# A third tap of layer 0's depthwise convolution moved to ScalarE, with an accumulating transfer in place of one add

## The chip, the cores and the metric

The kernel runs on one core of a Trainium2 chip. The metric is the device time of one execution in microseconds (us). All times are of float32 work: both layers compute in float32 (layer 1 splits its matmul operands into float32r halves).

## What is computed

The input x is (2, 768, 64, 64). Layer 0 is a gated state-space block on the group-normalised x, with 1536 inner channels (12 groups of 128):

```python
x = hs @ in_proj_w.T                       # 768 -> 1536 channels
xs = conv3x3_depthwise(x, conv_w) + conv_b # 9 taps for each channel, zero padding
xs = xs * sigmoid(xs)
dt, Bs, Cs = split(xs_seq @ x_proj_w.T, [R, R + DSTATE])   # R = 48, DSTATE = 4
delta = softplus(dt @ dt_w + dt_b)
states = scan over all 4096 positions of a*s + b, a = exp(delta * A), b = delta * u * Bs
y = sum over 4 states (states * Cs) + D * u
y = layernorm(y) * ln_g + ln_b
x = x + y @ out_proj_w.T                   # 1536 -> 768 channels
```

Layer 1 is a channel attention with two 768 x 768 projections. The change does not touch it.

## The kernel before

Layer 0 works in chunks of 8 image rows (512 positions): 8 chunks for each of 2 images, so 16 chunks, and in each chunk 12 tiles, one for each group of 128 inner channels. That makes 192 tiles of 128 x 512. The whole of layer 0 is one software pipeline written out by hand: `for S in range(SLOTS)`, where each engine has its own list of what it does in slot S. A tile goes through its steps at fixed distances. Tile i has its input projection in slot i, its convolution in slot i+2, the last adds of the convolution in slot i+3, the product with B in slot i+16, its scan in slot i+17, the sum over states in slot i+18, the statistics of the layer norm in slot i+19. The output projection of a chunk runs over slots 31 to 42 after the chunk's first slot. Each engine's queue is in order, and semaphores hold the engines together. In this text "slot 3" means a slot whose number leaves 3 when divided by 12; a chunk of 12 slots is a period in which everything recurs.

In one slot the engines do this:

- TensorE: the input projection of the new tile (6 matmuls, L564, into the one bank `p_in`), half an output projection (6 matmuls, L580, into the one bank `p_op`), in every second slot the sums of the layer norm. In slot 3 the small products that give dt, B and C (L675 just before it, L570, then L534); in slots 3, 7 and 11 the four products L534 that give dt for four tiles, in two pairs. The second pair waits until the first pair's softplus is done. Each output projection but the first waits until VectorE has taken the one before out of `p_op` (L952, `x_res`).
- VectorE: two scans (L917) and their products with C (L923), in odd slots the scaling of an output tile and the residual add (L945, L952), three convolution taps (L938), the two other scans and products, and three more taps, the last of which writes the sum to the tile's column of `uy`. In slot 8 it also works out the layer norm's factor.
- ScalarE: the centre tap, which starts the sum in the PSUM bank `p_cv` (L768); the square for the layer norm (L774); two taps as plain products into the buffer `conv_part` (CT, L715), with the skip product D * u (L785) between them; then the exponentials of the scan (L706, `p_da`, two before each pair of scans) and the copies of the scan's last state (L711). After them the copy of the new tile out of `p_in` (L739, L743, L747). In slots 2, 6 and 10 it applies SiLU to four tiles, in slots 3, 7 and 11 softplus to four tiles (L729), each with two loads of the function table.
- GpSimd: an accumulating transfer that adds two of the four states' products onto the other two (`g_ring`, L871, 512 KB), the two adds of ScalarE's products onto `uy` (L876, L879), delta * u (L883), its product with B for all four states (L889), and two more adds (L893, L897).

```python
def product(i, n):
    wait(act, s_conv, 2 * (i - 1) + n + 1)
    nc.scalar.activation(rows(CT[:, n]), win_view(i, 2, 1 + n), ACT.Copy,
                         scale=cwt[:, i % K, 7 + n:8 + n]).then_inc(s_ct, 1)
```

So each product waits until GpSimd has added the same product of the tile before. After ScalarE's part of slot S is done, VectorE's scans of slot S+1 can begin: the first exponential of the next tile (`decay(i, 0)`) is the last but one thing in ScalarE's slot.

## Time and profile before

| what | value |
|---|---|
| median of three runs | 3775.08 us (3770.55 to 3781.36) |
| the profiled execution: its own time, its span | 3775.21 us, 3773.4 us |
| TensorE busy over the span | 3440.0 us, 91% |
| VectorE | 2915.9 us, 77% |
| ScalarE | 2353.5 us, 62% |
| GpSimd | 2344.4 us, 62% |
| mean busy share of the DMA engines, layer 0 in its steady part | 0.55 |

The busy shares are means over both layers. Layer 0's pipeline runs from about 118 us to 2760 us of the span. Only there does the change act, and only while there are tiles to convolve, to about 2585 us. Times below are counted from the span's start. A row of the timeline has the start, the duration, engine, line, operation, the names and shapes, the count, and in brackets the idle time of that engine before it with what ended it.

### The profile page before, as it was taken

What the parts mean: (1) busy time and instruction counts of PE and PEld (TensorE: products, weight loads), DVE (VectorE), ACT (ScalarE), POOL (GpSimd) and SP (SyncE); (2) the same over time, 40 slices, a digit from 0 to 9 for tenths busy, and PEclk for the clock granted to TensorE, in tenths of its full rate; (3) what the DMA queues carried; (4) which work ended last, traced back from release to release, by engine and by line L of the source; (5) the groups of instructions that cost most, each with busy time, mean ns of one, the idle gap of its engine ahead of it and who ended that gap; (6) DMA issues with size and microseconds to landing.
All of it is one profiled execution on the core that took longest, in us unless ns stands there. A gap on an engine that the chain in (4) does not pass through costs nothing. (4 is left out here: it accounts for less than half of the span.)

```text
span 3773.4 us, 39046 instructions
## 1 busy us (share of the span) xinstructions
PE 3440.0 (91%) x10696; PEld 1731.0 (46%) x10696; DVE 2915.9 (77%) x4082; ACT 2353.5 (62%) x4094; POOL 2344.4 (62%) x1557
## 2 busy tenths in 40 slices
PE   4876799999999899999999999997879999999999
PEld 4422233333334344333333333332337867767787
DVE  4469999999999989999999999998743345555532
ACT  1356777788777767777777777777534555432211
POOL 0148888898889978988888889888820001112111
PEclk7888899999999999999999999998999999999999
DMA  7244455655556544555555555555532223356564
GB/s 281 88 143 107 102 139 132 166 137 144 145 130 170 131 126 133 144 147 146 150 134 144 147 147 149 136 140 156 130 108 78 65 82 99 111 185 198 198 195 154
DMA packets 217034, 529.85 MB, mean 140 GB/s; under 512 B 24728, under 2 KB 45784, under 8 KB 213872
## 3 DMA queue, kind: packets, MB, share of 16 engines
q1 hardware_dynamic: 173808, 376.32, 31.7%
q0 software_dynamic: 43008, 151.02, 18.3%
q8 instruction: 88, 1.44, 0.2%
q14 instruction: 130, 1.06, 0.1%
HBM read 346.11 MB, written 80.48 MB: 113 GB/s over the span
## 5 line engine op out<-in xcount | busy, mean ns | idle before, releaser
L564 PE MATMUL p_in<-xn,win_v 128*128 128x512 f32 (+1 forms) x2304 | 1062.5, 610 | 103.2 <-ACT halo L747 64.7
L580 PE MATMUL p_op<-uy,wout_ring 128*128 128x512 f32 x2160 | 1019.9, 622 | 83.4 <-DVE x_res L952 83.4
L917 DVE TENSOR_TENSOR_SCAN p_da<-p_da,state,g_ring 128x512 f32<-128x512 f32 x672 | 827.4, 1277 | 110.2 <-ACT p_da L706 74.6
L889 POOL TENSOR_TENSOR g_ring<-du,B_bc 128x2048 f32<-128x2048 f32 x192 | 870.6, 4534 | 15.9 <-DMA B_bc<-bc_scratch 0.9
L938 DVE SCALAR_TENSOR_TENSOR p_cv<-win_v,conv_w,p_cv 128x512 f32<-128x512 f32 x960 | 723.0, 753 | 88.5 <-ACT p_cv L768 67.5
L564 PEld LDWEIGHTS p_in<-xn,win_v 128*128 128x128 f32 x2304 | 442.2, 197 | 696.2 <-issue 696.2
L580 PEld LDWEIGHTS p_op<-uy,wout_ring 128*128 128x128 f32 x2160 | 413.5, 198 | 680.0 <-issue 568.1
L706 ACT ACTIVATE p_da<-delta,A 128x512 f32<-128x512 f32 x768 | 499.5, 682 | 12.5 <-ACT state L711 0.2
L923 DVE TENSOR_TENSOR g_ring<-p_da,C_bc 128x512 f32<-128x512 f32 x768 | 487.3, 676 | 0.0
L1370 PE MATMUL banks<-x_split,w_split 128*128 128x512 f32 x1152 | 464.2, 403 | 24.1 <-DMA ident<-in_ident_d 19.9
L1372 PE MATMUL banks<-x_split,w_split 128*128 128x512 f32 x1152 | 452.0, 392 | 0.0
L1371 PE MATMUL banks<-x_split,w_split 128*128 128x512 f32 x1152 | 451.5, 392 | 0.0
L876 POOL TENSOR_TENSOR uy<-uy,conv_part 128x512 f32<-128x512 f32 x192 | 256.0, 1333 | 259.2 <-DVE uy L938 259.2
L1215 POOL DMA_DIRECT2D q_scratch<-q_ring x96 | 51.9, 540 | 535.9 <-DVE q_ring L1635 535.7
L715 ACT ACTIVATE conv_part<-win_v,conv_w 128x512 f32<-128x512 f32 x384 | 273.4, 715 | 15.2 <-POOL uy L876 5.1
L1370 PEld LDWEIGHTS banks<-x_split,w_split 128*128 128x128 f32 x1152 | 218.0, 189 | 116.9 <-issue 38.9
L879 POOL TENSOR_TENSOR uy<-uy,conv_part 128x512 f32<-128x512 f32 x192 | 244.5, 1273 | 29.0 <-POOL uy L876 2.2
L711 ACT ACTIVATE state<-p_da 128x2 f32<-128x2 f32 x384 | 65.3, 170 | 304.3 <-DVE g_ring L923 301.9
L897 POOL TENSOR_TENSOR uy<-uy,g_ring 128x512 f32<-128x512 f32 x192 | 243.8, 1270 | 15.1
L893 POOL TENSOR_TENSOR g_ring<-g_ring 128x512 f32<-128x512 f32 x192 | 244.1, 1272 | 12.4 <-DMA g_ring<-g_ring 12.3
L883 POOL TENSOR_TENSOR du<-delta,uy 128x512 f32<-128x512 f32 x192 | 248.7, 1295 | 0.0
L1223 POOL DMA_DIRECT2D out<-x_ring x96 | 51.8, 540 | 311.1 <-DVE x_ring L1579 305.8
(212 smaller groups left out, 4283.6 us busy)
## 6 DMA issues: line engine op xcount, KB each, us to landing
g_ring<-g_ring POOLq DMA_DIRECT2D x192, 512.0 KB, 5.6
win_v<-in_win SPq DMA_DIRECT2D x192, 384.0 KB, 3.1
wout_ring<-wout_scratch SPq DMA_DIRECT2D x184, 384.0 KB, 4.0
x_ring<-x_scratch SPq DMA_DIRECT2D x192, 256.0 KB, 2.7
q_scratch<-q_ring POOLq DMA_DIRECT2D x96, 256.0 KB, 2.4
x_split<-q_scratch SPq DMA_DIRECT2D x96, 256.0 KB, 3.3
out<-x_ring POOLq DMA_DIRECT2D x96, 256.0 KB, 2.9
x_res<-in_x SPq DMA_DIRECT2D x90, 256.0 KB, 4.6
```

The source lines that it names most:

```text
L564: last = nc.tensor.matmul(p_in[:, 0:n], WR[:, i % NW, t, :], XN[:, t, off:off + n], start=(t == 0), stop=(t == XT - 1))
L580: last = nc.tensor.matmul(p_op[:], OR[:, e % NO, k - h * HALF, :], ucol(c * K + k), start=(k == 0), stop=(k == K - 1))
L706: nc.scalar.activation(p_da[:, n % 2, :], DL[:, i % ND, :], ACT.Exp, scale=At[:, j * NS + n:j * NS + n + 1]).then_inc(s_da, 1)
L715: nc.scalar.activation(rows(CT[:, n]), win_view(i, 2, 1 + n), ACT.Copy, scale=cwt[:, i % K, 7 + n:8 + n]).then_inc(s_ct, 1)
L876: nc.gpsimd.tensor_tensor(ucol(b), ucol(b), CT[:, 0], ALU.add).then_inc(s_conv, 1)
L889: nc.gpsimd.tensor_tensor(G[:, i % NG], DU[:].unsqueeze(1).broadcast_to([P, NS, N]), BB[:], ALU.mult).then_inc(s_dbu, 1)
L917: nc.vector.tensor_tensor_scan(bank, bank, G[:, i % NG, n, :], init, ALU.mult, ALU.add)\
L923: nc.vector.tensor_tensor(G[:, i % NG, n], p_da[:, n % 2, :], CB[:, n], ALU.mult).then_inc(s_cm, 1)
L938: nc.vector.scalar_tensor_tensor(rows(dst), win_view(i, dy, dx), cwt[:, j, 3 * dy + dx:3 * dy + dx + 1], rows(p_cv[:]), ALU.mult, ALU.add) ...
L1370: nc.tensor.matmul(bank(m), WX[:, m, q, 0, :], hi(h), start=(q == 0), stop=False)
L1371: nc.tensor.matmul(bank(m), WX[:, m, q, 0, :], lo(h), start=False, stop=False)
L1372: last = nc.tensor.matmul(bank(m), WX[:, m, q, 1, :], hi(h), start=False, stop=(q == XT - 1))
```

## The change

One more tap goes from VectorE to ScalarE. VectorE keeps five taps (rows 0 and 1 of the 3 x 3 window without the centre), ScalarE makes all three products of row 2. Products 0 and 1 are added by a transfer that accumulates (`conv_part` onto `conv_part`, 256 KB), which GpSimd issues between its product with B and the add L893. In the next slot GpSimd adds this sum and product 2 onto `uy`: two adds as before. Two semaphores of the layer norm are merged into one to free one for the transfer.

```diff
-        CT = sb("conv_part", [P, 2, N])
+        CT = sb("conv_part", [P, 3, N])
...
-        TAPS = [(dy, dx) for dy in range(3) for dx in range(3) if (dy, dx) not in ((1, 1), (2, 1), (2, 2))]
+        TAPS = [(dy, dx) for dy in range(3) for dx in range(3) if (dy, dx) != (1, 1) and dy < 2]
...
                 def product(i, n):
-                    wait(act, s_conv, 2 * (i - 1) + n + 1)
-                    nc.scalar.activation(rows(CT[:, n]), win_view(i, 2, 1 + n), ACT.Copy,
-                                         scale=cwt[:, i % K, 7 + n:8 + n]).then_inc(s_ct, 1)
+                    if n == 0:
+                        wait(act, s_conv, 2 * i - 1)
+                    elif n == 1:
+                        wait(act, s_cf, 16 * i)
+                    else:
+                        wait(act, s_conv, 2 * i)
+                    nc.scalar.activation(rows(CT[:, n]), win_view(i, 2, n), ACT.Copy,
+                                         scale=cwt[:, i % K, 6 + n:7 + n]).then_inc(s_ct, 1)
...
                     if b is not None:
                         product(b, 1)
+                        product(b, 2)
...
                     b = tile(S, L_CONV + 1)
                     if b is not None:
-                        pool.wait_ge(s_ct, 2 * b + 1)
+                        pool.wait_ge(s_cf, 16 * (b + 1))
                         pool.wait_ge(s_tap, len(TAPS) * (b + 1))
                         nc.gpsimd.tensor_tensor(ucol(b), ucol(b), CT[:, 0], ALU.add).then_inc(s_conv, 1)
-                        pool.wait_ge(s_ct, 2 * b + 2)
+                        pool.wait_ge(s_ct, 3 * b + 3)
                         pool.wait_ge(s_conv, 2 * b + 1)
-                        nc.gpsimd.tensor_tensor(ucol(b), ucol(b), CT[:, 1], ALU.add).then_inc(s_conv, 1)
+                        nc.gpsimd.tensor_tensor(ucol(b), ucol(b), CT[:, 2], ALU.add).then_inc(s_conv, 1)
...
+                    t = tile(S, L_CONV)
+                    if t is not None:
+                        pool.wait_ge(s_ct, 3 * t + 2)
+                        nc.gpsimd.dma_start(CT[:, 0], CT[:, 1], accum_op=ALU.add).then_inc(s_cf, 16)
                     if y is not None:
                         pool.wait_ge(s_ns1[y % NG], 16 * (y // NG + 1))
                         nc.gpsimd.tensor_tensor(gi[:, 0], gi[:, 0], gi[:, 1], ALU.add).then_inc(s_ns2, 1)
```

GpSimd's queue in the steady part, as it was before the change, for one slot from its transfer of the states' products to its last add:

```order
L871 DMA g_ring<-g_ring 128x1024
L876 TENSOR_TENSOR uy<-uy,conv_part 128x512
L879 TENSOR_TENSOR uy<-uy,conv_part 128x512
L883 TENSOR_TENSOR du<-delta,uy 128x512
L889 TENSOR_TENSOR g_ring<-du,B_bc 128x2048
L893 TENSOR_TENSOR g_ring<-g_ring 128x512
L897 TENSOR_TENSOR uy<-uy,g_ring 128x512
```

The same slot after the change:

```order
L876 DMA g_ring<-g_ring 128x1024
L881 TENSOR_TENSOR uy<-uy,conv_part 128x512
L884 TENSOR_TENSOR uy<-uy,conv_part 128x512
L888 TENSOR_TENSOR du<-delta,uy 128x512
L894 TENSOR_TENSOR g_ring<-du,B_bc 128x2048
L899 DMA conv_part<-conv_part 128x512
L902 TENSOR_TENSOR g_ring<-g_ring 128x512
L906 TENSOR_TENSOR uy<-uy,g_ring 128x512
```

One issue is new, L899. Between it and the add that waits for its landing (L881 of the next slot) stand two adds and the issue L876.

ScalarE's queue in a slot 6 (the SiLU slot), before, from the centre tap to the end of SiLU's table loads:

```order
L768 ACTIVATE p_cv<-win_v,cols,conv_w 128x512
L774 ACTIVATE sq<-uy 128x512
L715 ACTIVATE conv_part<-win_v,conv_w 128x512
L785 ACTIVATE uy<-uy,cols 128x512
L715 ACTIVATE conv_part<-win_v,conv_w 128x512
L711 ACTIVATE state<-p_da 128x2
L706 ACTIVATE p_da<-delta,A 128x512 x2
L825 ACT_TABLE_LOAD
L825 ACTIVATE uy<-uy 128x2048
L826 ACT_TABLE_LOAD
```

After the change:

```order
L772 ACTIVATE p_cv<-win_v,cols,conv_w 128x512
L778 ACTIVATE sq<-uy 128x512
L720 ACTIVATE conv_part<-win_v,conv_w 128x512
L789 ACTIVATE uy<-uy,cols 128x512
L720 ACTIVATE conv_part<-win_v,conv_w 128x512 x2
L711 ACTIVATE state<-p_da 128x2
L706 ACTIVATE p_da<-delta,A 128x512 x2
L830 ACT_TABLE_LOAD
L830 ACTIVATE uy<-uy 128x2048
L831 ACT_TABLE_LOAD
```

The third product stands ahead of the state's copy and of the exponentials, so all that follows in the slot is moved back by it. On VectorE the third of the taps after the second pair of scans is gone (L938 x2 and the one to `uy` become one and the one to `uy`).

## Rows read from the trace of the kernel before

**Rows 1.** Busy time of each engine over one chunk, slot 9 to slot 9.
```profile
1915.80:2073.00 157.20, 150.04 (x391) 59.23 (x391) 149.85 (x193) 124.17 (x215) 139.72 (x85) 0.98 0.56 144
```
**Rows 2.** Waits (us in total, times, longest): two lines from 118 to 2590, then three over one chunk.
```profile
PE p_op L580 <- DVE x_res L952: 55.3, 17, 5.4
...
DVE p_cv L938 <- ACT p_cv L768: 67.5, 18, 9.9
...
POOL uy L876 <- DVE uy L938: 9.2, 9, 1.2
DVE p_da L917 <- ACT p_da L706: 5.3, 4, 2.1
POOL g_ring L871 <- DVE g_ring L923: 4.7, 3, 2.6
```
**Rows 3.** Timeline of slot 3 of that chunk: ScalarE, VectorE.
```profile
1993.13 0.60 ACT L792 ACTIVATE x_dbl<-p_dt 128x512 f32<-128x512 f32 x1 [1.17 <-PE p_dt L570]
...
1994.61 2.47 DVE L917 TENSOR_TENSOR_SCAN p_da<-p_da,state,g_ring 128x512 f32<-128x512 f32 x2 [2.15 <-ACT p_da L706]
...
2002.50 2.47 DVE L917 TENSOR_TENSOR_SCAN p_da<-p_da,state,g_ring 128x512 f32<-128x512 f32 x2 [2.01 <-ACT p_da L706]
```
**Rows 4.** Groups of instructions by line and shape, 700 to 2500.
```profile
L938 DVE SCALAR_TENSOR_TENSOR p_cv<-win_v,conv_w,p_cv 128x512 f32<-128x512 f32 x682 | 513.5, 753 | 23.2 <-ACT p_cv L768 8.7
...
L871 POOL DMA_DIRECT2D g_ring<-g_ring x136 | 118.7, 873 | 72.0 <-DVE g_ring L923 68.6 <-issue 3.2
```
**Rows 5.** Timeline of ScalarE, slots 6 and 7.
```profile
2027.28 0.78 ACT L768 ACTIVATE p_cv<-win_v,cols,conv_w 128x512 f32<-128x512 f32 x1 [0.82 <-DVE uy L938]
...
2028.61 0.72 ACT L715 ACTIVATE conv_part<-win_v,conv_w 128x512 f32<-128x512 f32 x1
2029.24 0.71 ACT L785 ACTIVATE uy<-uy,cols 128x512 f32<-128x512 f32 x1
...
2045.61 1.27 ACT L729 ACTIVATE delta<-p_dt,cols 128x512 f32<-128x512 f32 x2
...
2048.21 1.27 ACT L729 ACTIVATE delta<-p_dt,cols 128x512 f32<-128x512 f32 x2 [0.48 <-PE p_dt L534]
...
2050.99 1.30 ACT L706 ACTIVATE p_da<-delta,A 128x512 f32<-128x512 f32 x2
```
**Rows 6.** Timeline of VectorE (starts of slots 7 and 8) and TensorE (slots 7 and 9).
```profile
2039.12 2.47 DVE L917 TENSOR_TENSOR_SCAN p_da<-p_da,state,g_ring 128x512 f32<-128x512 f32 x2 [0.37 <-ACT p_da L706]
...
2052.11 2.46 DVE L917 TENSOR_TENSOR_SCAN p_da<-p_da,state,g_ring 128x512 f32<-128x512 f32 x2
...
2047.05 1.13 PE L534 MATMUL p_dt<-x_dbl,dt_w 48*128 48x512 f32 x4
...
2072.89 7.67 PE L580 MATMUL p_op<-uy,wout_ring 128*128 128x512 f32 x11 [4.04 <-DVE x_res L952]
```
**Rows 7.** GpSimd's and SyncE's timeline, slots 3 to 6.
```profile
1994.31 1.27 POOL L893 TENSOR_TENSOR g_ring<-g_ring 128x512 f32<-128x512 f32 x1
...
1995.22 0.33 SPq L495 DMA_DIRECT2D B_bc<-bc_scratch  x1
...
2000.65 1.26 POOL L876 TENSOR_TENSOR uy<-uy,conv_part 128x512 f32<-128x512 f32 x1 [1.22 <-DVE uy L938]
...
2027.32 1.26 POOL L876 TENSOR_TENSOR uy<-uy,conv_part 128x512 f32<-128x512 f32 x1 [1.06 <-DVE uy L938]
```
**Rows 8.** Landings: L871's, 700 to 2500; then the page's issues and a group of layer 1.
```profile
DMA to landing us min/median/max: 4.5/5.9/10.7
...
q_scratch<-q_ring POOLq DMA_DIRECT2D x96, 256.0 KB, 2.4
...
L1215 POOL DMA_DIRECT2D q_scratch<-q_ring x96 | 51.9, 540 | 535.9 <-DVE q_ring L1635 535.7
```
**Rows 9.** GpSimd's timeline in the pipeline's fill, slots 10 and 11.
```profile
335.94 1.26 POOL L876 TENSOR_TENSOR uy<-uy,conv_part 128x512 f32<-128x512 f32 x1 [0.62 <-DVE uy L938]
...
348.47 1.26 POOL L876 TENSOR_TENSOR uy<-uy,conv_part 128x512 f32<-128x512 f32 x1 [0.65 <-DVE uy L938]
```

More of the change, by code:

```diff
@@ L327, in layer0 @@
          s_delta, s_du, s_dbu, s_da, s_scan, s_scp, s_cm, s_skip,
-         s_ns2, s_y, s_sq, s_ln, s_ls, s_mean, s_msq, s_e2, s_var, s_vare, s_lv, s_rs0, s_nt,
+         s_ns2, s_y, s_sq, s_ln, s_ls, s_cf, s_msq, s_e2, s_var, s_vare, s_lv, s_rs0, s_nt,
          s_rstd, s_op, s_ov, s_bn, s_pad, s_zero, s_oa, s_xe, s_xf, s_ct, s_conv) = (sem("q_" + n) for n in (
              "xn inp row rowev vev hin hout tap0 tap silu xp xd dt delta du dbu da "
-             "scan scp cm skip ns2 y sq ln ls mean msq e2 var vare lv rs0 nt rstd op ov bn pad "
+             "scan scp cm skip ns2 y sq ln ls cf msq e2 var vare lv rs0 nt rstd op ov bn pad "
              "zero oa xe xf ct conv").split())
@@ L507, in _ @@
                         sp.wait_ge(s_tap, len(TAPS) * NT)
-                        sp.wait_ge(s_ct, 2 * NT)
+                        sp.wait_ge(s_ct, 3 * NT)
                         for m in range(4):
@@ L662, in _ @@
                         nc.tensor.matmul(norm_bank(c)[:, 0, :], pick[64:P, :], LS[64:P, :], start=True, stop=True)\
-                          .then_inc(s_mean, 1)
+                          .then_inc(s_e2, 1)
                         nc.tensor.matmul(norm_bank(c)[:, 1, :], pick[0:64, :], LS[0:64, :], start=True, stop=True)\
@@ L713, in product @@
                 def product(i, n):
-                    wait(act, s_conv, 2 * (i - 1) + n + 1)
-                    nc.scalar.activation(rows(CT[:, n]), win_view(i, 2, 1 + n), ACT.Copy,
-                                         scale=cwt[:, i % K, 7 + n:8 + n]).then_inc(s_ct, 1)
+                    if n == 0:
[6 more added lines that the diff above has]
+                                         scale=cwt[:, i % K, 6 + n:7 + n]).then_inc(s_ct, 1)
                 def row_out(i):
                     wait(act, s_tap, len(TAPS) * (i - NV + 1))
-                    wait(act, s_ct, 2 * (i - NV + 1))
+                    wait(act, s_ct, 3 * (i - NV + 1))
                     act.wait_ge(s_row, first_rows(i))
@@ L735, in evacuate @@
                     wait(act, s_tap, len(TAPS) * (i - NV + 1))
-                    wait(act, s_ct, 2 * (i - NV + 1))
+                    wait(act, s_ct, 3 * (i - NV + 1))
                     if k > 0:
@@ L753, in _ @@
                     if c is not None:
-                        act.wait_ge(s_mean, c + 1)
-                        act.wait_ge(s_e2, c + 1)
+                        act.wait_ge(s_e2, 2 * (c + 1))
                         nc.scalar.activation(LS[:], norm_bank(c)[:, 0, :], ACT.Square).then_inc(s_msq, 1)
@@ L902, in _ @@
                             wait(pool, s_tap, len(TAPS) * (i - NV + 1))
-                            wait(pool, s_ct, 2 * (i - NV + 1))
+                            wait(pool, s_ct, 3 * (i - NV + 1))
                             nc.gpsimd.memset(VS[:, i % NV, 0 if k == 0 else ROWS + 1, :], 0.0).then_inc(s_zero, 1)
@@ L971, in _ @@
                     if c is not None:
-                        vec.wait_ge(s_e2, c + 1)
+                        vec.wait_ge(s_e2, 2 * (c + 1))
                         vec.wait_ge(s_msq, c + 1)
```

## The prediction

> **What bounds the kernel now.** I read the busy times over one chunk first. In 157.20 us TensorE is busy for 150.04, VectorE for 149.85, GpSimd for 139.72, ScalarE for 124.17, at a granted clock of 0.98 [rows 1]. So neither TensorE nor VectorE is the bound alone: each has some 7 us of idle time in a chunk, and what matters is who waits for whom. The waits say it [rows 2]: TensorE waits for `x_res`, VectorE's emptying of `p_op`, 55.3 us in all. One long wait of 4.04 us in slot 9 [rows 6] comes back in every steady chunk (13 of them make nearly all of the 55.3). VectorE in turn waits 5.3 us in a chunk for ScalarE's exponentials (`p_da`).
>
> The timeline joins these. In slot 3 ScalarE waits 1.17 us for TensorE's product L570 and then copies it out; VectorE, which waits for what ScalarE does behind it, stands 2.15 us, and 2.01 us more at the start of slot 4 [rows 3]. So slot 3 ties ScalarE and VectorE to TensorE. From there to slot 9 VectorE is late by 4.04 us against TensorE. From slot 9 to the next slot 3 TensorE works nearly without idle time. The period of 157.2 is therefore TensorE's stretch from slot 9 to slot 3 and a chain through VectorE and ScalarE from slot 3 to slot 9. Only a shorter chain from slot 3 to slot 9 shortens a chunk, by at most 4.04 us.
>
> **VectorE loses a tap.** One tap is 0.753 us [rows 4], so 0.75 us a slot, 9.0 a chunk. Slot 9's `x_res` comes before that slot's taps; between the ties of slot 3 and `x_res` of slot 9 lie the late taps of slots 3 to 8. That of slot 3 is lost in the 2.01 us wait. Five would remain, 3.8 us, if nothing else held VectorE.
>
> **ScalarE gains a product.** A product moves what is behind it by 0.63 us (start of L715 to the next start [rows 5]). Slots 3, 4 and 5 have waits that hide it: 1.17 us ahead of L792 in slot 3, and waits for VectorE's tap sum such as the 0.82 us before L768 of slot 6 [rows 3, 5]. In slots 6 and 7 nothing hides it. Between L768 of slot 6 and VectorE's scan of slot 7, which waits 0.37 us for ScalarE [rows 5, 6], ScalarE works through. So VectorE's saving up to slot 6 (the taps of slots 4 and 5, 1.5 us) is cut there.
>
> **GpSimd gains an issue and a landing.** Its own work is 139.72/12 = 11.64 us a slot [rows 1]. What the issue costs no row shows for this form. The nearest rows are the 512 KB accumulation at 0.873 us [rows 4] and the plain 256 KB store at 0.540 [rows 8]. I take 0.87, since the new issue accumulates too and has as many rows; the other end is 0.54. That makes 12.51 us a slot, under the 13.1 of a chunk's slot.
>
> The landing: L871, 512 KB, lands 4.5 us after its issue at least, 5.9 in the median, 10.7 at most; the 256 KB store lands after 2.4 [rows 8]. The new transfer moves half of L871's bytes, and I take half of what L871 has over the store (4.5 - 2.4 = 2.1) as its price for bytes and adding: between 2.4 and 4.5, about 3.4 with free DMA engines, and more beside other transfers. The add that needs it comes 0.87 + 2 x 1.27 + 0.87 = 4.3 us after the start of the issue (its own issue, two adds as in [rows 7], L871). So it lands in time when the engines are free. But SyncE loads `B_bc` at 1995.22, just after GpSimd would issue slot 3's transfer (at 1994.3, where L893 begins now [rows 7]), and that is the longest load of the chunk. With L871's longest landing less its least (6.2 us) as a bound, slot 3's transfer lands between 3.4 and 9.6 us after its issue. I take 7.5.
>
> The Trainium skill puts a lower price on the landing ("DMA: Bandwidth & Descriptors", section "Anatomy of one DMA — SWDGE (gpsimd) path"): about 2.0 us and the bytes over 436 GB/s. An estimate by it is 2.6 us for 256 KB, and 3.2 for L871's 512 KB, where the row has 4.5 to 10.7. So the trace disagrees with it for an accumulating transfer beside this traffic; by it the sum would be that of the early case below.
>
> **From slot 3 to slot 9, worked out.** Early case (all land in time): GpSimd's adds in slot 4 begin at 2000.65 - 0.75 = 1999.9 [rows 7], two slots of 12.51 later and with some 1.2 us of waits for VectorE that stay, slot 6's begin at about 2026.1 (2027.32 before). ScalarE's first product, which waits for that add, begins some 0.9 earlier than 2028.61 [rows 5]. The third product takes 0.63 of it back: VectorE's scan of slot 7 begins 0.3 earlier. Slot 7's third product makes the first softplus pair, which ended at 2046.88, 0.3 later. TensorE's second pair of L534 waits for it and started at 2047.05 [rows 5, 6], so it goes 0.2 later, and with it the second softplus (2048.21) and the exponential for slot 8 (2050.99). VectorE's scan of slot 8 (2052.11) had about 0.3 us of room behind that, so it begins at the old time. Only slot 8's tap (and the time up to `x_res`) is left: 0.8 us a chunk.
>
> Late case: slot 3's transfer lands at about 2001.9, GpSimd's adds of slot 4 begin then, and two slots of 12.51 lead to 2026.9 or 2027.1 in slot 6, as late as before. The two extra products stay: softplus +1.3, TensorE's second pair +1.2, the scan of slot 8 +0.9, less slot 8's tap 0.75: 0.15 us a chunk longer.
>
> Over 13 chunks that is -10 us or +2 us. I take -2, nearer to the late case, since `B_bc` is loaded at that place in each chunk.
>
> **The rest.** In the fill (slots up to 30) no output projection loads TensorE. There a slot is 348.47 - 335.94 = 12.53 us with a GpSimd wait of 0.65 [rows 9]; its work is 11.88, with the issue 12.75, so 0.22 us a slot for some nine slots: +2. VectorE waits 18 times, 67.5 us, for ScalarE's centre tap [rows 2], in the first slots of the fill. In most of them ScalarE itself waits for TensorE, and the product is hidden; in about four it isn't: 4 x 0.63 = +2.5.
>
> Sum against the profiled execution (3775.21, as good as the median 3775.08): 3775.2 - 2 + 2 + 2.5 = **3778 us**. A difference under 0.3% (11.3 us) can't be told from none.
>
> **The rivals.**
> - The saving reaches TensorE: ScalarE's third product finds room, and landings are early. Five taps are 3.8 us of the 4.04: 13 x 3.8 = 49 us less, 3778 without the -2 gives about 3731. For it: VectorE is busy 95% of a chunk. Against it: the 0.37 us wait for ScalarE in slot 7, already there before, and the tie of L534 to softplus. A part of it (over 0.85 us a chunk) is enough to be seen. Together 0.23.
> - GpSimd becomes the bound, slower. Place: its add L881 behind the landing. The price: with 12.51 us of work a slot it reaches the 13.1 of a slot when the add waits 0.59 us on the mean, a landing of 4.9 us. At L871's median of 5.9 the wait is 1.6: 14.1 us a slot, 12 us a chunk, over some 14 chunks +168 us, 3943; at 5.2 us it is 13.4 a slot, +3.7 a chunk, 3827. For it: the median landing of L871. Against it: half the bytes, and 3.4 us with free engines. Chance 0.20.
> - ScalarE becomes the bound, slower: the product counts in full in all six SiLU and softplus slots, 3.8 us a chunk, 14 chunks: +53, 3828. For it: no wait in slots 6 and 7 but 0.48 us. Against it: ScalarE is busy only 124 of 157 us [rows 1], and TensorE's waits in slot 3 reset it. Chance 0.12.
> - The forecast, within 0.3% of before: 0.45. The skill's price for landings (3770, the early sum) lies inside it with 0.1 of these.
>
> **The numbers.** Faster by over 0.3%: 0.23. Within 0.3%: 0.45. Slower: 0.20 + 0.12 = 0.32. The range leaves out the far half of the first rival (below 3752) and the far end of the two slower ones (above 3825), about 1 in 10 on each side.
>
> **What the changed profile would show.** VectorE's busy time in a chunk is 141 instead of 150, ScalarE's 132, GpSimd's 150. TensorE's wait for `x_res` in slot 9 stays, between 2.5 and 4.2 us: were it gone, the first rival is right. VectorE waits more for `p_da`, at the starts of slots 7 and 8 above all. The new transfer lands after 3 to 4 us in most slots and late in slot 3. GpSimd has a wait for `conv_part` there, and if it has one in most slots, it is the bound. TensorE gets a new wait for softplus (L534 on `delta`) in slot 7. What would make the forecast wrong most: a landing as long as L871's, an issue at 0.54 (0.33 us a slot less for GpSimd), or a phase of the SyncE loads that hits other slots than 3.

## The result, and the profile after

| | before | changed |
|---|---|---|
| median | 3773.14 us (3770.55 to 3781.36, 4 runs) | 3883.26 us (3880.52 to 3892.64, 4 runs) |
| ratio to before | | 1.0292, 95% interval 1.0268 to 1.0317 |
| profiled execution: own time, span | 3775.21, 3773.4 us | 3892.64, 3890.9 us |
| TensorE, VectorE, ScalarE, GpSimd busy | 3440.0, 2915.9, 2353.5, 2344.4 us | 3467.5, 2778.7, 2452.6, 2513.3 us |

The change costs 110 us, where 3778 us (3752 to 3825) was forecast. The profiled execution is the longest of the four, 9 us over the median. The spans differ by 117.5 us, and layer 0 accounts for all of it: the last tile's centre tap starts at 2703.3 instead of 2585.5 us.

One chunk of the changed kernel, slot 9 to slot 9, answers to [rows 1], in the same columns: length, busy time of PE, PEld, DVE, ACT and POOL with their instructions, granted clock, DMA share, GB/s.

```profile
1995.72:2162.25 166.53, 151.86 (x391) 59.50 (x391) 141.52 (x181) 130.19 (x227) 150.22 (x97) 0.97 0.64 155
```

A chunk takes 166.5 us instead of 157.2 (others 162.5 to 167.5). The busy times are the forecast ones, 141 for VectorE and 150 for GpSimd, so the work was counted rightly. The waits were not. They answer to [rows 2]: four lines of all engines from 700 to 2500, then GpSimd's in that one chunk:

```profile
DVE p_da L926 <- ACT p_da L706: 240.3, 121, 7.6
...
ACT conv_part L720 <- POOL uy L881: 100.2, 65, 5.1
POOL uy L881 <- DMA conv_part<-conv_part: 88.1, 31, 5.0
PE p_in L564 <- ACT halo L752: 56.4, 26, 4.7
...
POOL uy L881 <- DMA conv_part<-conv_part: 9.6, 4, 4.7
POOL g_ring L876 <- DVE g_ring L932: 2.2, 2, 1.7
POOL uy L881 <- DVE uy L947: 0.9, 2, 0.4
```

GpSimd now waits for the landing of the new transfer, 9.6 us in the chunk. Its 150.22 us of work and 12.7 of waits leave 3.6 of the 166.53, the short times between its instructions (e6 says more on these). ScalarE's first product waits behind GpSimd's add, and TensorE waits for ScalarE's evacuation (`halo`), a wait that was 9.9 us in the same stretch before. GpSimd's timeline shows where it starts, in slots 3 to 5:

```profile
2072.89 4.53 POOL L894 TENSOR_TENSOR g_ring<-du,B_bc 128x2048 f32<-128x2048 f32 x1
2077.37 0.86 POOL L899 DMA_DIRECT2D conv_part<-conv_part  x1
2077.97 1.55 POOL L902 TENSOR_TENSOR g_ring<-g_ring 128x512 f32<-128x512 f32 x1
...
2086.42 1.26 POOL L881 TENSOR_TENSOR uy<-uy,conv_part 128x512 f32<-128x512 f32 x1 [4.72 <-DMA conv_part<-conv_part]
...
2094.89 0.87 POOL L899 DMA_DIRECT2D conv_part<-conv_part  x1
...
2102.39 1.26 POOL L881 TENSOR_TENSOR uy<-uy,conv_part 128x512 f32<-128x512 f32 x1 [3.17 <-DMA conv_part<-conv_part]
```

The issues of SyncE beside them (the second row holds the two halves of `C_bc`, of which the second is issued at 2094.8):

```profile
2077.51 0.32 SPq L495 DMA_DIRECT2D B_bc<-bc_scratch  x1
...
2088.45 6.68 SPq L502 DMA_DIRECT2D C_bc<-bc_scratch  x2
```

The transfer of slot 3 was issued 0.14 us ahead of the `B_bc` load and landed after 9.0 us; that of slot 4 was issued 0.1 us behind the second half of `C_bc` and landed after 7.4. Over all steady chunks slot 3's took 7.6 to 9.2 us and slot 4's 6.6 to 8.1 (one chunk at the change of image apart), slot 11's 3.5 to 8.2, most others 3.3, some up to 5.3.

This meeting of slot 3's transfer with the `B_bc` load is no chance of the phase. SyncE may load `B_bc` only when the product L894 of slot 3 has read the old one, and the same product is the last thing ahead of L899 in GpSimd's queue. In 14 of 15 chunks the load is issued 0.07 to 0.12 us behind the product's end, here at 2077.42. In the kernel before it was 0.86 to 1.00 us in nine of 15, since there the load waited for its source in memory longer than for the product.

The view of the transfer's own line, 700 to 2500:

```profile
L899 POOL DMA_DIRECT2D conv_part<-conv_part x130: 842/864/898, 701.6 to 2494.0; - x130
...
  POOL uy L881: 88.1, 31
...
DMA to landing us min/median/max: 3.2/3.3/9.2
```

ScalarE's and TensorE's timelines show the lateness on its way, in slots 5 to 7:

```profile
2098.44 0.63 ACT L778 ACTIVATE sq<-uy 128x512 f32<-128x512 f32 x1 [1.31 <-POOL uy L906]
2103.68 0.72 ACT L720 ACTIVATE conv_part<-win_v,conv_w 128x512 f32<-128x512 f32 x1 [4.61 <-POOL uy L881]
...
2108.65 5.39 PE L564 MATMUL p_in<-xn,win_v 128*128 128x512 f32 x12 [0.29 <-ACT halo L752]
...
2126.10 7.67 PE L564 MATMUL p_in<-xn,win_v 128*128 128x512 f32 x12 [4.54 <-ACT halo L752]
```

TensorE loses 4.54 us ahead of slot 7's input projection, waiting for ScalarE's evacuation in slot 6, and then 2.28 more: the projection's six matmuls, which the trace records as twelve, take 7.67 us behind this stall and 5.39 a slot earlier. The windows view has a granted clock of 0.50 from 2126.1 to 2130.0, of 0.77 for the ten microseconds from 2126.10 and of 1.00 for the next ten.

### The profile page after: what moved, and what is told of

The parts are those of the page before. It is cut to its first block and busy times, and to the rows that moved or that the text cites. A ratio compares the mean times of both kernels' runs of the same rounds, so it can differ in the third digit from the quotient of the medians.

```text
span 3890.9 us, 39222 instructions
## 1 busy us (share of the span) xinstructions
PE 3467.5 (89%) x10696; PEld 1739.1 (45%) x10696; DVE 2778.7 (71%) x3890; ACT 2452.6 (63%) x4286; POOL 2513.3 (65%) x1749
## 5 line engine op out<-in xcount | busy, mean ns | idle before, releaser
L564 PE MATMUL p_in<-xn,win_v 128*128 128x512 f32 (+1 forms) x2304 | 1104.0, 630 | 179.0 <-ACT halo L752 120.2
L580 PE MATMUL p_op<-uy,wout_ring 128*128 128x512 f32 x2160 | 1007.7, 616 | 70.6 <-DVE x_res L961 70.6
L894 POOL TENSOR_TENSOR g_ring<-du,B_bc 128x2048 f32<-128x2048 f32 x192 | 870.2, 4532 | 16.5 <-DMA B_bc<-bc_scratch 1.6
L564 PEld LDWEIGHTS p_in<-xn,win_v 128*128 128x128 f32 x2304 | 456.2, 204 | 800.7 <-issue 800.6
L580 PEld LDWEIGHTS p_op<-uy,wout_ring 128*128 128x128 f32 x2160 | 408.8, 196 | 659.7 <-issue 564.5
L947 DVE SCALAR_TENSOR_TENSOR p_cv<-win_v,conv_w,p_cv 128x512 f32<-128x512 f32 x768 | 577.5, 752 | 100.8 <-ACT p_cv L772 86.6
L720 ACT ACTIVATE conv_part<-win_v,conv_w 128x512 f32<-128x512 f32 x576 | 390.1, 711 | 148.6 <-POOL uy L881 148.4
L881 POOL TENSOR_TENSOR uy<-uy,conv_part 128x512 f32<-128x512 f32 x192 | 273.0, 1422 | 172.2 <-DMA conv_part<-conv_part 158.4
L902 POOL TENSOR_TENSOR g_ring<-g_ring 128x512 f32<-128x512 f32 x192 | 294.5, 1534 | 13.3 <-DMA g_ring<-g_ring 13.3
L1379 PEld LDWEIGHTS banks<-x_split,w_split 128*128 128x128 f32 x1152 | 217.3, 189 | 117.1 <-issue 37.1
L884 POOL TENSOR_TENSOR uy<-uy,conv_part 128x512 f32<-128x512 f32 x192 | 244.7, 1275 | 27.8 <-POOL uy L881 0.4
L1381 PEld LDWEIGHTS banks<-x_split,w_split 128*128 128x128 f32 x1152 | 217.2, 189 | 47.1
```

What stands on the lines that cost most here:

```text
L564: last = nc.tensor.matmul(p_in[:, 0:n], WR[:, i % NW, t, :], XN[:, t, off:off + n], start=(t == 0), stop=(t == XT - 1))
L580: last = nc.tensor.matmul(p_op[:], OR[:, e % NO, k - h * HALF, :], ucol(c * K + k), start=(k == 0), stop=(k == K - 1))
L720: nc.scalar.activation(rows(CT[:, n]), win_view(i, 2, n), ACT.Copy, scale=cwt[:, i % K, 6 + n:7 + n]).then_inc(s_ct, 1)
L894: nc.gpsimd.tensor_tensor(G[:, i % NG], DU[:].unsqueeze(1).broadcast_to([P, NS, N]), BB[:], ALU.mult).then_inc(s_dbu, 1)
L902: nc.gpsimd.tensor_tensor(gi[:, 0], gi[:, 0], gi[:, 1], ALU.add).then_inc(s_ns2, 1)
L947: nc.vector.scalar_tensor_tensor(rows(dst), win_view(i, dy, dx), cwt[:, j, 3 * dy + dx:3 * dy + dx + 1], rows(p_cv[:]), ALU.mult, ALU.add) ...
```

## The experiments

Every ratio below is to the kernel before, measured beside it. First the four that undo one part of the change each.

**e1: both broadcast loads small.** From the second chunk on the loads of `B_bc` and `C_bc` move 8 values a partition each, and the scan works with the first chunk's B and C.

```diff
-sp.dma_start(BB[:]..., bc_d[c, 0:NS]...partition_broadcast(P))
+sp.dma_start(BB[:, 0, 0:8], bc_d[c, 0, 0:8].partition_broadcast(P))      # if c > 0
-sp.dma_start(CB[:, 2 * h:2 * h + 2]..., bc_d[c, NS + 2 * h:NS + 2 * h + 2]...)
+sp.dma_start(CB[:, 2 * h, 0:8], bc_d[c, NS + 2 * h, 0:8].partition_broadcast(P))
```

> The changed kernel, but the loads of B_bc and C_bc (1 MB each in a chunk) move 4 KB from the second chunk on; the scan then works with the first chunk's B and C. Theory A (the transfer of slots 3 and 4 lands late behind these two loads, and the 4.7 and 3.2 us that GpSimd waits in each chunk for it are the loss): 3765 to 3795 us. Theory B (GpSimd's own work with the new issue, 12.5 us a slot, is the loss, whenever it lands): still 3860 or more. Theory C (ScalarE's third product, 0.63 us in each of the six long slots of a chunk): still about 3830.

Measured: 3800.7 us, 1.0068 (1.0051 to 1.0085). Slot 3's transfer lands after 3.9 us, slot 4's after 3.3, and a chunk takes 156.1 us. (In three chunks they still land after 6.1 to 7.3 and 5.8 to 5.9.) So 83 of the 110 us are gone, fewer than theory A asked for: 3800.7 lies 6 us above its range. The rest is not in the steady chunks, which are 1 us shorter than before.

**e2: no transfer.** Product 1 is left out of the sum.

```diff
-                        wait(act, s_cf, 16 * i)
+                        wait(act, s_ct, 3 * i - 1)
-                        pool.wait_ge(s_cf, 16 * (b + 1))
+                        pool.wait_ge(s_ct, 3 * b + 1)
-                        nc.gpsimd.dma_start(CT[:, 0], CT[:, 1], accum_op=ALU.add).then_inc(s_cf, 16)
```

> The changed kernel without the new transfer: product 1 is made but left out of the sum, GpSimd adds products 0 and 2. Theories A and B: 3760 to 3785 us, as both the issue and the landing are gone. Theory C: about 3830, since ScalarE still makes three products. Beside the small loads of the other kernel this gives what the issue alone costs: by A almost nothing between the two, by B some 80 us.

Measured: 3740.4 us, 0.991 (0.9896 to 0.9925). Five taps with three products save 36 us when the transfer is absent, 20 more than any of the three theories had.

**e3: the transfer issued ahead of the product with B.** ScalarE makes product 1 next to product 0. The computation is complete.

```diff
+                    t = tile(S, L_CONV)
+                    if t is not None:
+                        pool.wait_ge(s_ct, 3 * t + 2)
+                        nc.gpsimd.dma_start(CT[:, 0], CT[:, 1], accum_op=ALU.add).then_inc(s_cf, 16)
                     if i is not None:   # the product with B
```

> The changed kernel with the same work, but the transfer is issued ahead of GpSimd's product with B, not behind it, and ScalarE makes product 1 ahead of the skip product. The add that needs the landing then comes 8.8 us after the issue, not 4.3, so landings of 7 to 8 us are in time. Theory A: 3765 to 3795 us. Theory B: 3860 or more, as GpSimd has as much to do. Theory C: about 3830.

Measured: 3773.0 us, 0.9994 (0.9985 to 1.0004). A transfer in slot 4 still takes 5.5 to 8.1 us here, but almost nobody waits for it (1.2 us from 700 to 2500); slot 3's lands after 3.3, with the `B_bc` load 5.5 us behind it. The landing waits are gone, and the gain of e2 is gone as well: something other than the landing costs 33 us. Two things are candidates: GpSimd's time for the issue, and that the early issue waits for ScalarE's product 1 (45.9 us in 28 waits in the same stretch). e6 takes the second away.

**e4: five taps alone**, with two products and no transfer; tap (2, 0) is left out of the sum.

```diff
-        ... if (dy, dx) not in ((1, 1), (2, 1), (2, 2))]
+        ... if (dy, dx) != (1, 1) and dy < 2]
```

> The kernel before with one tap (2,0) left out of the convolution: what VectorE's saving is worth when nothing is added elsewhere. If VectorE's chain from slot 3 to slot 9 is all that makes TensorE wait, 13 chunks x 3.8 us = 49 us less, 3725 us. If ScalarE's slots 6 and 7 cut the saving, as the forecast says, 0.8 to 1.5 us a chunk: 3755 to 3764 us.

Measured: 3728.2 us, 0.9875 (0.9861 to 0.989), near the 3725 of a saving through VectorE's chain alone, so VectorE's tap is worth 48 us, and ScalarE's third product takes 12 of it back (e2 less e4). TensorE's stall in slot 9 is shorter in e2, and its matmuls are faster behind it in most chunks; the timeline of e2 at two such places:

```profile
1892.65 6.90 PE L580 MATMUL p_op<-uy,wout_ring 128*128 128x512 f32 x12 [2.92 <-DVE x_res L957]
...
2047.40 5.42 PE L580 MATMUL p_op<-uy,wout_ring 128*128 128x512 f32 x12 [2.93 <-DVE x_res L957]
```

Before, the stall was 4.04 us and eleven of these matmuls took 7.67 us [rows 6], twelve 8.0 to 8.4. Over the nine places of e2 with a stall of 2.6 to 2.9 us twelve took 5.42 to 8.47, 6.65 on the mean. The shorter stall and the faster matmuls are some 2.5 us, about what a chunk of e2 is shorter (2.3).

**e6: the issue alone**, at the changed kernel's place. To e2 a transfer of the same size between two spare buffers is added. Only the next such issue would have to wait for it, which never happened from 700 to 2500, and it waits for no product.

```diff
-                        pool.wait_ge(s_ct, 3 * t + 2)
-                        nc.gpsimd.dma_start(CT[:, 0], CT[:, 1], accum_op=ALU.add).then_inc(s_cf, 16)
+                        wait(pool, s_cf, 16 * t)
+                        nc.gpsimd.dma_start(SPR[:, 0], SPR[:, 1], accum_op=ALU.add).then_inc(s_cf, 16)
```

> The kernel without the accumulating transfer (3740.4 us; product 1 is left out of the sum), to which an accumulating transfer of the same size between two spare buffers is added at the changed kernel's place, behind the product with B. Nothing but the next issue of the same kind waits for its landing. Theory, GpSimd's work costs (0.87 us more in each slot, 10.4 us a chunk, of which only a part was idle): as the kernel with the early issue, 3765 to 3780. Rival, only landings and their waits cost: 3740 to 3747. If the transfers beside it slow the other loads, more than 3780.

Measured: 3775.2 us, 0.9994 (0.9985 to 1.0003). The issue costs 35 us although nobody waits for what it moves. The windows view of one chunk and GpSimd's waits in it:

```profile
2072.15:2228.19 156.04, 148.85 (x391) 58.92 (x391) 141.23 (x181) 130.13 (x227) 150.47 (x97) 0.99 0.69 165
```

```profile
POOL g_ring L879 <- DVE g_ring L935: 1.0, 1, 1.0
POOL uy L884 <- DVE uy L950: 0.8, 2, 0.4
```

150.47 us of work and 1.8 of waits are 152.3, and what is left of 156.04, 3.8 us, are the short times between its instructions: in each slot 0.14 us between the two adds onto `uy`, and twice 0.08. They are in [rows 1, 2] too: 139.72 of work and 9.2 + 4.7 of waits leave 3.6 of the 157.20. That work, waits and short times add up to the chunk holds for any engine. What tells the bound is that the waits are nearly nothing: TensorE has 7.2 us without work in this chunk and VectorE 14.8, GpSimd waits for 1.8. GpSimd's queue is full in e6, and the chunk is as long as its list.

A rival would be the added traffic, whoever issues it. e7 has none of it and is slower still, and e8 has the bytes of e3 with half the issues and takes 15 us less. What the bytes cost beside that, in the 18 us between e2 and e8, is not shown.

**e7: three adds on GpSimd**, no transfer, complete.

```diff
+                        for n in range(3):
+                            pool.wait_ge(s_ct, 3 * b + n + 1)
+                            wait(pool, s_conv, 3 * b + n)
+                            nc.gpsimd.tensor_tensor(ucol(b), ucol(b), CT[:, n], ALU.add).then_inc(s_conv, 1)
```

> The full computation with no transfer at all: ScalarE makes the three products, and GpSimd adds all three onto uy. GpSimd has 11.64 + 1.27 = 12.91 us of work in a slot, against 12.5 with the issue and 11.64 before, and no landing is waited for. Theory, GpSimd's work per slot sets the time once it comes over some 12 us: 12.91 of a slot of 13.1 gives 3785 to 3810. Rival, only landings cost and GpSimd's work is hidden under 13.1 us: 3740 to 3750, faster than before.

Measured: 3846.7 us, 1.0188 (1.0172 to 1.0203), beyond both expectations. The reason is in the same two views:

```profile
2118.36:2280.04 161.68, 150.97 (x390) 59.27 (x391) 141.56 (x181) 131.62 (x227) 155.57 (x97) 0.98 0.54 140
```

```profile
POOL g_ring L871 <- DVE g_ring L922: 0.4, 1, 0.4
POOL uy L878 <- DVE uy L937: 0.4, 1, 0.4
```

155.57 + 0.8 leave 5.3 of 161.68, more than in e6 since there are two gaps of 0.14 us in a slot now. No transfer of products exists here, and GpSimd waits for almost nothing: 5.1 us more work and 1.6 more of short times, less 1.0 of waits, are the 5.6 us by which the chunk is longer than e6's. My expectation had set its room at 13.1 - 12.91 us a slot and left the short times out, as the prediction had.

**e8: one transfer for two tiles**, complete. An issue took 0.86 us for 256 KB and 0.87 for 512 KB, so pairs halve the cost. Five product buffers; the issue is early, in the odd tile's slot, and GpSimd adds both sums in the slot behind it.

```diff
-        CT = sb("conv_part", [P, 3, N])
+        CT = sb("conv_part", [P, 5, N])
...
+                    if t is not None and t % 2:
+                        pool.wait_ge(s_ct, 3 * t + 2)
+                        nc.gpsimd.dma_start(CT[:, 0:2], CT[:, 2:4], accum_op=ALU.add).then_inc(s_cf, 16)
```

> The full computation, with one accumulating transfer of 512 KB for each pair of tiles in place of two of 256 KB, issued early in the odd tile's slot (five buffers for the products). An issue took 0.86 us for 256 KB and 0.87 for 512 KB, so GpSimd has 11.64 + 0.43 = 12.07 us in a slot instead of 12.5. Theory, GpSimd's work costs: between the kernel without the transfer (3740.4) and the one with an early issue for each tile (3773.0), so about 3755, faster than before by 0.5%. Rival, what costs is the landing that GpSimd and ScalarE wait for: the larger transfer lands later (4.5 us and more), so 3773 or above.

Measured: 3758.1 us, 0.9949 (0.9936 to 0.9962), half a per cent faster than the kernel before. Its transfer's view and its chunk:

```profile
L897 POOL DMA_DIRECT2D conv_part<-conv_part x68: 877/877/1192, 715.3 to 2475.4; - x68
...
DMA to landing us min/median/max: 4.5/6.1/8.4
```

```profile
1908.95:2064.78 155.83, 147.36 (x391) 58.10 (x391) 141.23 (x181) 130.09 (x227) 144.89 (x91) 1.00 0.66 166
```

The landing is long and no add waits for it. GpSimd has 8.8 us of waits in this chunk, so it is not the bound here.

**e5 and e9: which load.** In e5 only the `C_bc` loads are small, in e9 only the `B_bc` load, each with e1's edit.

> The changed kernel, in which from the second chunk on only the C_bc loads move almost nothing (8 values a partition; the scan's products use the first chunk's C, so the output is not the reference's); the B_bc load keeps its size. With both loads small the changed kernel took 3800.7 us instead of 3883.3. Theory: both loads delay a transfer, B_bc that of slot 3 and the second half of C_bc that of slot 4, and slot 4's wait comes on top of slot 3's: with C_bc small the wait of slot 4 (about 4.7 us) is gone and slot 3's (about 3) stays, so about half of the 83 us comes back, 3835 to 3850. Rival, only B_bc's load counts (as the prediction had it): 3880 or more, nothing comes back. Second rival, slot 3's lateness is absorbed by the slots behind it and only slot 4's is paid for: about 3800.

Measured: 3876.2 us, 1.0264 (1.025 to 1.0278). The rival holds: almost nothing comes back, 7 us between the medians, which the spread of the runs hardly resolves. Slot 4's transfer lands after 5.9 to 6.5 us.

> The changed kernel, in which from the second chunk on only the B_bc load moves almost nothing (8 values a partition; the product with B uses the first chunk's B, so the output is not the reference's); the C_bc loads keep their size. Both loads small gave 3800.7 us, C_bc alone 3876.2. In that run slot 4's transfer still landed after 5.9 to 6.5 us. Theory: the B_bc load delays the transfers of both slots, 3 and 4 (it is a MB that starts just behind slot 3's issue), and GpSimd's two waits behind them are what the 83 us are: 3800 to 3815, landings of slots 3 and 4 under 5 us. Rival, the two loads share the delay of slot 4, so that with C_bc full slot 4's transfer is still late: 3830 to 3860.

Measured: 3802.3 us, 1.0074 (1.006 to 1.0088). `B_bc` alone gives back 81 of the 83 us, and slot 3's transfer lands after 3.9 us and slot 4's after 3.3 to 4.3 in most chunks, though `C_bc` has its full size. So slot 4's delay follows from slot 3's: GpSimd, 4.72 us late, issues it onto the second half of `C_bc` and its neighbours. In e9 it is issued 2.4 us behind that load in most chunks. One chunk of e9, with 1.9 us of GpSimd's waits, is as e6's:

```profile
1932.87:2088.96 156.09, 147.40 (x390) 58.19 (x391) 141.25 (x181) 130.13 (x227) 150.49 (x97) 1.00 0.66 159
```

**e10: two buffers for products 0 and 1**, complete: `CT[:, 2 * (i % 2) + n]` for these, `CT[:, 4]` for product 2, and waits that lie a tile further back.

> The full computation. The changed kernel with two buffers for each of products 0 and 1, used in turn, so that ScalarE's first two products no longer wait until GpSimd has taken those of the tile before; issue and landing stay where they are. Theory, GpSimd's own queue sets the time (in the chunk of the kernel with the spare transfer its work is 150.5 us, the short times between its instructions 3.8, its waits 1.8, of 156.04): its wait for the landings stays, so the time stays, 3870 to 3890. Rival, the late landing costs because ScalarE's product waits for the buffer and the evacuation behind it is late for TensorE: without that wait most of the 83 us of the late landings comes back, 3800 to 3830.

Measured: 3877.4 us, 1.027 (1.0255 to 1.0285). It lies where the theory had it, but does not separate it from the rival, since ScalarE now waited for product 2's single buffer (84.3 us for L884 from 700 to 2500).

**e11: one add less.** GpSimd adds product 2 for 8 of 512 columns.

```diff
-nc.gpsimd.tensor_tensor(ucol(b), ucol(b), CT[:, 2], ALU.add)
+nc.gpsimd.tensor_tensor(ucol(b)[:, 0:8], ucol(b)[:, 0:8], CT[:, 2, 0:8], ALU.add)
```

> The changed kernel, in which GpSimd adds product 2 for 8 of its 512 columns only (the rest of product 2 is left out of the sum): 1.27 us less work in a slot less what a tiny add takes, some 14 us less in a chunk; transfers, issues and waits stay. Theory, GpSimd's queue is the bound: the wait of some 8 to 10 us in slots 4 and 5 is made up within a few slots, and the time falls to where TensorE bounds again, 3740 to 3765, 120 us and more below the changed kernel. Rival, the landing waits cost through ScalarE and TensorE, whatever GpSimd has to do: 3840 or more.

Measured: 3769.0 us, 0.9985 (0.9976 to 0.9994), 114 us below the changed kernel and 4 above the theory's range. One chunk has 137.67 us of GpSimd's work in 155.89, with 3.5 of waits for landings. From 700 to 2500 those waits fell to 43.4 us, as the whole phase moved: the `B_bc` load is issued 3.5 us behind slot 3's transfer in most chunks, which lands after 3.3 us. So with less work on GpSimd the loss is gone, but work and late landing went together, and the run doesn't show what a late landing costs a queue with room.

**e12: e8 with products 0 and 1 ahead of the copy of `x_dbl`**, complete. It is e8 with the block `product(b, 0)`, `product(b, 1)` moved up over that copy.

> The full computation. The kernel with one 512 KB transfer for a pair of tiles (3758.1 us), in which ScalarE makes products 0 and 1 ahead of its copy of x_dbl in slot 3, so that GpSimd's issue there doesn't wait for them (4.5 us a chunk in that kernel, in four waits). Theory, GpSimd's waits are paid for in part, the rest of the chunk being TensorE's: 155.8 us a chunk falls by 0.5 to 1, 3745 to 3752. Rival, ScalarE's copy of x_dbl comes later by up to 1.3 us, TensorE's products behind it too, and nothing is won: 3758 to 3770.

Measured: 3758.7 us, 0.9958 (0.9944 to 0.9971), the same as e8 and in the rival's range. The issue's waits for products fell only from 69.8 to 59.1 us (700 to 2500), so taking that part away gains nothing.

**e13: no product waits for an add**, complete: products 0 and 2 have two buffers, product 1 is made last.

```diff
-                        wait(act, s_conv, 2 * i - 1)     # product 0
+                        wait(act, s_conv, 2 * i - 3)
-                        wait(act, s_conv, 2 * i)         # product 2
+                        wait(act, s_conv, 2 * i - 2)
-                        product(b, 1)
                         product(b, 2)
+                        product(b, 1)
-                        pool.wait_ge(s_ct, 3 * t + 2)
+                        pool.wait_ge(s_ct, 3 * t + 3)
```

> The full computation. In the run with two buffers for products 0 and 1 ScalarE's wait had only moved to product 2, which kept one buffer (84 us waited for L884 in 1800, against 100 us for L881 in the changed kernel). Here products 0 and 2 have two buffers each, and product 1, whose buffer only the transfer reads, is made last. So no product waits for a GpSimd add of the tile before, only product 1 for the landing. Theory, GpSimd's own queue (150 us of work a chunk, and waits for the landings on top) sets the time: 3865 to 3890. Rival, ScalarE's wait for the buffers carries the lateness to TensorE: 3800 to 3840.

Measured: 3828.8 us, 1.014 (1.012 to 1.0161), in the rival's range. Slot 3's transfer lands as late as ever (8.2 to 9.5 us, the change of image apart). One chunk of it, and GpSimd's waits from its list of all waits:

```profile
2104.01:2264.97 160.96, 151.94 (x390) 59.82 (x391) 141.50 (x181) 129.70 (x227) 150.44 (x97) 0.97 0.66 160
```

```profile
POOL uy L881 <- DMA conv_part<-conv_part: 6.2, 2, 4.5
...
POOL uy L884 <- ACT conv_part L720: 0.4, 1, 0.4
POOL uy L881 <- DVE uy L947: 0.2, 1, 0.2
```

150.44 + 6.8 leave 3.7 of 160.96. So both theories hold a part. GpSimd has the work of e6 and 5.0 us more of waits, and the chunk is 4.9 us longer: the landing waits are paid in full. But ScalarE's waits had a share in how the other engines stand to the loads: here slot 4's issue falls 2.7 us behind the second half of `C_bc` instead of onto it, and the second wait is the smaller part of the 6.2 us (9.6 before). The run as a whole gains 54 us over the changed kernel; whether all of it comes from that phase isn't shown.

**e14: the `B_bc` load behind the landing**, complete.

```diff
                         wait(sp, s_dbu, K * c)
+                        if tile(S, L_CONV) is not None:
+                            sp.wait_ge(s_cf, 16 * (tile(S, L_CONV) + 1))
                         sp.dma_start(BB[:]...
```

> The full computation. The changed kernel, in which SyncE issues the B_bc load of slot 3 only when the conv_part transfer of that slot has landed (one wait more on SyncE). Landing of slot 3's transfer then 3.3 to 4 us after its issue instead of 7.6 to 9.2; the B_bc load begins some 3.5 us later and, at 6.1 us from issue to landing, lands at about 2087, before the product with B that needs it began in slot 4 (2090.41). Theory, that one coincidence of slot 3 makes both late landings: 3800 to 3815, as with the B_bc load made small. Rival, the B_bc load only moves onto the transfers behind it (the g_ring one of slot 4 or conv_part's), and GpSimd waits there instead: 3840 to 3890.

Measured: 3805.7 us, 1.0078 (1.0061 to 1.0095). The load keeps its size and only starts later, 3.3 us behind the issue of slot 3's transfer, which lands after 3.3 us; slot 4's lands after 3.3 to 4.5 in most chunks, and 78 us come back, as the theory had it. GpSimd's waits in one chunk (157.46 us, 150.40 of work):

```profile
POOL g_ring L896 <- DMA B_bc<-bc_scratch: 1.4, 1, 1.4
POOL g_ring L878 <- DVE g_ring L934: 1.0, 1, 1.0
POOL uy L883 <- DMA conv_part<-conv_part: 0.7, 1, 0.7
```

## Why the prediction was wrong

The path from the kernel before to the changed one in terms of medians: five taps -48 (e4), the third product +12 (e2), the issue +35 (e6), the landings outside the coincidence and the issue's own wait for its products +27 (e9 less e6; the `B_bc` load is small in e9 too), the coincidence with the `B_bc` load +81 (the changed kernel less e9). They are differences of neighbouring medians, so they add up by construction, to 107 us against the 3776 us of the kernel before beside e4. That each size would be the same in another order is not shown.

- **"GpSimd gains an issue": the step that failed.** The issue was taken at 0.87 us and measured 0.864. The error was in what it was held against, "12.51 us a slot, under the 13.1 of a chunk's slot". The short times between GpSimd's instructions, 3.6 us a chunk, were left out. They stand in the rows as what work and waits leave of the chunk [rows 1, 2]. With them GpSimd's list is 150.2 + 3.6 = 153.8 us, and only 3.4 of 157.2 were left for all waits, not 7. The chunk of the changed kernel has 12.7 us of waits, and 153.8 + 12.7 is its 166.5. The rival "GpSimd becomes the bound" had the mechanism. It put the point from which it decides at 0.59 us of landing wait a slot; with the short times that point is 0.3. The sign named for it failed too: GpSimd was to be the bound if it waited for `conv_part` in most slots, and it is the bound with 31 such waits for 130 transfers.
- **"The landing": near in slot 3, incomplete behind it.** The usual landing was forecast at 3.4 and is 3.3 us; slot 3's at 7.5 and is 7.6 to 9.2, so that the add waits 4.72 us in the chunk shown where 3.2 (7.5 less 4.3) followed from the forecast. By the Trainium skill ("DMA: Bandwidth & Descriptors", section "Anatomy of one DMA — SWDGE (gpsimd) path") 256 KB would take an estimated 2.6 us; the rows have 3.2 at least, so the trace disagrees by 0.6 us. What the forecast did not do is move the rest of the chunk: slot 3's wait puts slot 4's issue onto the second half of `C_bc`, and 3.17 us more are waited. e9 and e14 show this second wait as a consequence of the first, e13 that the waits on ScalarE's side have a part in it. And it took the place of the `B_bc` load as given, 0.9 us behind the issue, where the load follows the end of GpSimd's own product.
- **"Late case: slot 3's transfer lands at about 2001.9 ... as late as before": failed with the first.** It let GpSimd stand still until the landing and counted two slots of 12.51 behind it, without the short times and without the second late landing. The measured late case is not +0.15 us but some 5 to 10 us a chunk.
- **"VectorE loses a tap" and "ScalarE gains a product": under-rated.** The early case gave 0.8 us a chunk. e2 shows 2.3 to 2.4 (154.8 instead of 157.2), of which the shorter stall is 1.1 and the faster matmuls behind it, 1.4 on the mean, are the rest (TensorE's busy time falls from 150.0 to 148.6 and 147.3 in two chunks). The term that was missing is the price of TensorE's clock behind a stall. The rival "the saving reaches TensorE" said 3731, and e4 and e2 bracket it from 3728 to 3740; it was right as to VectorE and came to nothing because of GpSimd. That e3, with its landings in time, took 3773.0 us, near the 3770 of the early case, is luck: a saving of 36 us where 10 were counted met a cost of 33 for the issue where GpSimd's share was put at 2.
- **"The rest".** For the fill +2 was forecast, from work alone. In the second and third chunk period the changed kernel loses 11 us against the kernel before. e9 loses 13 there against e6, which has the same work, but had gained 7 in the first. Of the 25 us between the profiles of these two (last tile's centre tap) 6 are in the first three periods, 8 at the change of image and 8 in the last one; most steady chunks are 156.1 in both. In the fill GpSimd stands up to 7.7 us for product 1 before it can issue (4 waits, 15.3 us in e9, from 230 to 560) and 22.9 us for landings. In e6 it has neither of these waits, but 37.8 us for VectorE, where e9 has 7.8. So it is argued, not shown, that an issue which waits and holds everything behind it in the queue is what costs there.
- **"TensorE gets a new wait for softplus in slot 7": another wait.** TensorE has a new one in slot 7, of 4.54 us, but for ScalarE's evacuation in slot 6, since a late add holds ScalarE's product and so everything behind it in ScalarE's slot. The forecast's other signs came: 141 us of VectorE's work, 130 of ScalarE's (132 forecast) and 150 of GpSimd's, and a stall of 2.9 us for `x_res`.

Left open: which transfers beside `C_bc` keep slot 4's landing at 5.9 to 6.5 us in e5, what the 27 us between e6 and e9 consist of, and what a single late landing costs when GpSimd has room.

## What to carry to other kernels

Add up an engine's queue as busy time, waits and the short times between instructions before you call it free: what the period leaves after the first two is not room. A transfer that is awaited in the next slot is priced by what is issued beside it, at the slot where that happens: a load 0.14 us behind it cost 4 us and more, the same load 3.3 us behind it nothing. Ask what releases that load, since two transfers that one event releases meet in each period. A wait for a landing moves all later issues, so the phase of the loads has to be gone through again. A transfer's issue cost counts for each instruction, so one large transfer for two tiles, issued early, beat two small ones (e8, 15 us below e3).

## What the runs showed of the hardware

- An accumulating transfer costs GpSimd 0.86 us to issue at 256 KB and 0.87 to 0.88 at 512 KB, both with 128 rows. At 256 KB it lands after 3.3 us in most slots, and after 7.6 to 9.2 when a 1 MB broadcast load is issued 0.1 us behind it, but after 3.2 to 3.7 when that load is issued 3.3 to 3.8 us behind it (e14) and 3.3 at 5.5 us (e3). The load itself lands in 6.1 us.
- Twelve matmul records of L564 took 5.39 us, and 7.67 us behind a stall of 4.54 us, with a granted clock of 0.50, the level of 1.2 GHz, in the first four microseconds behind it. Twelve of L580 took 5.42 to 8.47 us behind stalls of 2.9 us in e2, and 8.38 behind the one at 2162.25 of the changed kernel, with a granted clock of 0.50 from there to 2168.0. The Trainium skill ("TensorE: Matmul & The Clock Gate", section "Part 1: The HAM clock gate (the "warmup" mystery)") says that the clock is halved in an idle array and that activity releases it; the rows agree. So TensorE's stall of 2.9 us cost between itself (5.42 behind it) and twice itself (8.38, 3.0 us more than 5.42).
- GpSimd's queue has short times without work: 0.14 us between two adds of which the second needs the first's result, 0.08 at two other places of a slot, 3.6 us in a chunk of 12 slots (5.3 in e7, with three adds in a row).
- An instruction of GpSimd behind an issue starts before the issue's record ends and takes longer by about as much: L902 is 1.55 us there, and the same add is 1.27 in the kernel before, where no issue stands ahead of it. In sums of durations these overlaps must be left out.
